# Which engine sums the last low column, casts the values and takes the stabilisers' low part in an fp32 attention

## What is computed

```
scores = jnp.einsum('bhqd,bhkd->bhqk', q, k) * scale
attn = jax.nn.softmax(scores, axis=-1)
out = jnp.einsum('bhqk,bhkd->bhqd', attn, v)
out = out.transpose(0, 2, 1, 3).reshape(b, s, H * DH)
out = out @ w_out.T + residual
```

## Time and profile before

| | |
|---|---|
| median of three runs | 4191.82 us |
| the profiled execution | 4191.36 us |
| its span, first to last instruction | 4189.6 us |
| TensorE matmul | 3758.9 us, 90% |
| VectorE | 3392.4 us, 81% |
| GpSimd | 3042.9 us, 73% |
| ScalarE | 2623.1 us, 63% |

### The profile page before, as it was taken

One profiled execution on the slowest core, in us unless ns is written; L12 is line 12 of the kernel. 1 busy time (PEld: TensorE's weight loads), 2 busy tenths in 40 slices (PEclk: granted clock), 3 DMA queues, 4 the chain that ended last, 5 costly groups with the idle time before them and its releaser, 6 DMA issues. The chain is left out here.

```text
span 4189.6 us, 55316 instructions
## 1 busy us (share of the span) xinstructions
PE 3758.9 (90%) x17018; PEld 2903.6 (69%) x17018; DVE 3392.4 (81%) x4389; ACT 2623.1 (63%) x3395; POOL 3042.9 (73%) x2832
## 2 busy tenths in 40 slices
PE   7949977869999999999999999999999999979563
PEld 4635545548888888888888888888888888857321
DVE  6845548869999999999999999999999999946511
ACT  6723333337777777777777777777777777733221
POOL 2456765758888888888888888888888888820155
PEclk9969998979999999999999999999999999989676
DMA  7123437852224332242322423224232242046295
GB/s 271 47 65 60 67 78 244 274 160 63 61 58 89 65 65 60 57 92 62 66 59 59 93 60 67 60 57 91 62 66 59 63 88 61 20 160 221 73 248 111
DMA packets 332634, 396.27 MB, mean 95 GB/s; under 512 B 142541, under 2 KB 251922, under 8 KB 319284
## 3 DMA queue, kind: packets, MB, share of 16 engines
q1 hardware_dynamic: 307702, 362.22, 33.9%
q0 software_dynamic: 24640, 30.52, 4.2%
HBM read 232.47 MB, written 117.79 MB: 84 GB/s over the span
## 5 line engine op out<-in xcount | busy, mean ns | idle before, releaser
L1815 ACT ACTIVATE at_ph<-at_ps_s 128x1024 fp32r<-128x1024 f32 x1024 | 1052.7, 1028 | 637.0 <-PE at_ps_s L1864 621.3
L1724 DVE TENSOR_REDUCE at_mx<-at_ps_u 128x2 f32<-128x1024 f32 x1016 | 1239.8, 1220 | 157.5 <-PE at_ps_u L1847 122.1
L1744 DVE TENSOR_TENSOR at_pl<-at_ps_s,at_ph 128x1024 fp32r<-128x1024 f32 x1024 | 1245.8, 1217 | 18.5 <-ACT at_ps_s L1818 17.4
L1818 ACT ACTIVATE at_ps_s<-at_ps_s 128x1024 f32<-128x1024 f32 x1024 | 1032.2, 1008 | 32.6
L1653 POOL TENSOR_TENSOR at_part<-at_ph,at_vl 128x512 f32<-128x512 f32 x768 | 799.0, 1040 | 114.2 <-ACT at_ph L1815 90.2
L1661 POOL TENSOR_TENSOR at_acc<-at_acc,at_part 128x512 f32<-128x512 f32 x640 | 833.5, 1302 | 50.1
L1879 PE MATMUL at_ps_v<-at_ph,at_va 128*128 128x512 f32 x2048 | 812.2, 397 | 1.1 <-DVE at_pl L1744 1.1
L1880 PE MATMUL at_ps_v<-at_pl,at_va 128*128 128x512 f32 x2048 | 812.9, 397 | 0.0
L1882 PE MATMUL at_ps_v<-at_ph,at_vx 128*128 128x512 f32 x1152 | 456.2, 396 | 0.0
L1880 PEld LDWEIGHTS at_ps_v<-at_pl,at_va 128*128 128x128 f32 x2048 | 387.4, 189 | 90.4
L1863 PE MATMUL at_ps_s<-q,k 128*128 128x512 f32 x1024 | 410.9, 401 | 21.6 <-DVE at_pl L1744 19.5
(11 more groups left out here) (285 smaller groups left out, 5446.3 us busy)
## 6 DMA issues: line engine op xcount, KB each, us to landing
wgu<-Wgu_in SPq DMA_DIRECT2D x64, 384.0 KB, 5.1
qT<-pj_rot SPq DMA_DIRECT2D x32, 512.0 KB, 5.2
vT<-pj_vo SPq DMA_DIRECT2D x16, 1024.0 KB, 5.7
kT<-pj_rot SPq DMA_DIRECT2D x32, 512.0 KB, 3.2
k<-kT SPq DMA_DIRECT2D x32, 512.0 KB, 11.6
q<-qT SPq DMA_DIRECT2D x32, 512.0 KB, 9.5
at_q<-at_low SPq DMA_DIRECT2D x128, 128.0 KB, 2.3
at_vf<-vT SPq DMA_DIRECT2D x32, 512.0 KB, 8.7
```

The lines of the kernel that those rows point to most:

```text
L1724: dve.tensor_reduce(mx[:, qb % 2, 2 * i:2 * i + 2], maxima_at(base, j)[:, 0:2], X, ALU.max).then_inc(s["u_max"], 1)
L1744: dve.tensor_tensor(pl[:, n % NP], ps_s[:, n % 2], ph[:, n % NP].bitcast(F32), ALU.subtract)\
L1815: act.activation(ph[:, n % NP], ps_s[:, n % 2], ACT.Exp, scale=DH ** -0.5)\
L1818: act.activation(ps_s[:, n % 2], ps_s[:, n % 2], ACT.Exp, scale=DH ** -0.5)\
```

## The change

There are four edits that belong together. (1) `SUMS` goes from 7 to 8: all even chunks are summed by GpSimd, slot 7 included, and `NX` from 9 to 8: TensorE has no second own product in slot 7. The `fold` of a block, the copy of its output and `whole` move back by one slot. (2) The casts to the high part of the values go from GpSimd to ScalarE, in slots 15, 17, 19 and 21. (3) The subtraction for `ml` goes from VectorE to GpSimd, into slot 2 of each block, behind a wait for VectorE's reductions. (4) The own products are prepared with one small copy instead of two.

```diff
-        SUMS = PER - 1
+        SUMS = PER
         NX = 2 * PER - SUMS
-        TAIL = 3
+        TAIL = 4
...
-                if c == KC - 2:
-                    return NX - 1
                 return c // 2 if c % 2 == 1 else None
...
-                def split_values(g, hh, half, i):
-                    if i == 0:
-                        pool.wait_ge(s[f"v{hh}"], half * 16 + 16)
-                        if g > 0:
-                            pool.wait_ge(s["pv_done"], g * SLOTS + (NP - SLOTS))
-                    at = slice(i * VQ, (i + 1) * VQ)
-                    pool.tensor_copy(va[:, hh, at, 0:DH], vf[:, hh, at]).then_inc(s["vh_ready"], 1)
...
-                    pool.tensor_copy(vx[:, hh, 0:NX - 1, 0:1], vl0[:, hh, 1::2].unsqueeze(2)).then_inc(s["vx_ready"], 1)
-                    pool.tensor_copy(vx[:, hh, NX - 1:, 0:1], vl0[:, hh, KC - 2:KC - 1].unsqueeze(2)).then_inc(s["vx_ready"], 1)
+                    pool.tensor_copy(vx[:, hh, :, 0:1], vl0[:, hh, 1::2].unsqueeze(2)).then_inc(s["vx_ready"], 1)
...
-                        if c < KC - 4:
+                        if c < KC - 2:
                             to = acc[:]
...
+                def low_stabilisers(block_):
+                    pool.wait_ge(s["mg_ready"], 2 * (block_ + 1))
+                    pool.tensor_tensor(ml[:, block_ % NQB], mg[:], mh[:, block_ % NQB].bitcast(F32), ALU.subtract)\
+                        .then_inc(s["nm_ready"], 1)
...
                         first_sums(g, hh, n)
-                        if n % PER == 5 and g * NQB + n // PER > 0:
+                        if n % PER == 2 and g * NQB + n // PER + 1 < HEADS * NQB:
+                            low_stabilisers(g * NQB + n // PER + 1)
+                        if n % PER == 6 and g * NQB + n // PER > 0:
                             whole((g * NQB + n // PER - 1) // NQB, (n // PER - 1) % NQB)
...
-                            if i % 2 == 0:
-                                split_values(nxt, 1 - hh, pr + hh, i // 2)
-                            else:
+                            if i % 2 == 1:
                                 low_values(nxt, 1 - hh, i // 2)
...
-                    dve.wait_ge(s["mg_ready"], 2 * (base * NQB + (qb + 1)))
-                    dve.tensor_tensor(ml[:, qb], mg[:], mh[:, qb].bitcast(F32), ALU.subtract).then_inc(s["nm_ready"], 1)
...
+                def split_values(g, hh, half, i):
+                    if i == 0:
+                        act.wait_ge(s[f"v{hh}"], half * 16 + 16)
+                        if g > 0:
+                            act.wait_ge(s["pv_done"], g * SLOTS + (NP - SLOTS))
+                    at = slice(i * VQ, (i + 1) * VQ)
+                    act.activation(va[:, hh, at, 0:DH], vf[:, hh, at], ACT.Copy).then_inc(s["vh_ready"], 1)
...
-                        if n % PER == 2 and n > PER:
+                        i = n % SLOTS - SLOTS // 2 + 1
+                        if 0 <= i < 2 * NQB and i % 2 == 0 and 2 * pr + n // SLOTS + 1 < HEADS:
+                            split_values(2 * pr + n // SLOTS + 1, 1 - n // SLOTS, pr + n // SLOTS, i // 2)
+                        if n % PER == 3 and n > PER:
                             output(pr * 2 + (n - PER) // SLOTS, (n - PER) % SLOTS // PER)
...
-                        if n % PER == 0 and g * NQB + n // PER > 0:
+                        if n % PER == 1 and g * NQB + n // PER > 0:
                             fold(g * NQB + n // PER - 1)
```

More of the change, by code:

```diff
@@ L1472, in sums_before @@
                 return n // PER * SUMS + sum(own_product(c) is None for c in range(2 * (n % PER)))
+            VQ = KC // NQB
             def loaded(eng, name, hh, half, each):
@@ L1597, in _ @@
                     link(pool.memset(k2[i][MROW:MROW + 2, :].bitcast(F32), -1.0))
-                VQ = KC // NQB
-                def split_values(g, hh, half, i):
-                    if i == 0:
-                        pool.wait_ge(s[f"v{hh}"], half * 16 + 16)
-                        if g > 0:
-                            pool.wait_ge(s["pv_done"], g * SLOTS + (NP - SLOTS))
-                    at = slice(i * VQ, (i + 1) * VQ)
-                    pool.tensor_copy(va[:, hh, at, 0:DH], vf[:, hh, at]).then_inc(s["vh_ready"], 1)
                 def low_values(g, hh, i):
@@ L1688, in head @@
                             own_products(nxt, 1 - hh)
+                low_stabilisers(0)
                 for i in range(NQB):
-                    split_values(0, 0, 0, i)
                     low_values(0, 0, i)
@@ L1819, in pair @@
                             .then_inc(s["pf_ready"], 1)
-                        if n % PER == 2 and n > PER:
+                        i = n % SLOTS - SLOTS // 2 + 1
+                        if 0 <= i < 2 * NQB and i % 2 == 0 and 2 * pr + n // SLOTS + 1 < HEADS:
+                            split_values(2 * pr + n // SLOTS + 1, 1 - n // SLOTS, pr + n // SLOTS, i // 2)
+                        if n % PER == 3 and n > PER:
                             output(pr * 2 + (n - PER) // SLOTS, (n - PER) % SLOTS // PER)
-                        elif n == 2 and pr > 0:
+                        elif n == 3 and pr > 0:
                             output(pr * 2 - 1, NQB - 1)
+                for i in range(NQB):
+                    split_values(0, 0, 0, i)
                 for pr in range(PAIRS):
@@ L1872, in values @@
                             pe.wait_ge(s["v_split"], g * NQB + NQB)
-                            pe.wait_ge(s["vx_ready"], 2 * (g + 1))
+                            pe.wait_ge(s["vx_ready"], g + 1)
                         if c2 == 0:
```

## The result

The changed kernel took 4465.94 us (4460.43 to 4475.94, 4 runs) beside 4191.28 us for the kernel before on the same chip: ratio 1.0656, 95% interval 1.0634 to 1.0678. The forecast was 4212 in a range from 4190 to 4252. The direction was right; the loss is 275 us where 21 were forecast.

The account below looks back on a forecast made before the run. TensorE bounds before, GpSimd after: about 6 us of first idle, 31 heads of 87.7 (2718.7) and a last of 80.5 sum to 2805.2, 21 us more than 2784.1; 4191.4 + 21 gives 4212 us, range 4190 to 4252.

Parts of the forecast that it names:

- GpSimd's sum of 87.7 us a head: GpSimd's work in an attention head after the change, if it never idles: 87.7 us, 0.7 more than today's head.
- The whole of attention: All 32 heads, first product to last addition: 2805.2 us after against 2784.1 before, 21 us more.
- The pair of product and addition: GpSimd's cost for one chunk in a block: forecast to stay at 2.56 us.
- its bounds: Stabilisers' low part on GpSimd: between 0 and 0.3 us beyond the gap each, 1.2 us a head at most.
- The casts on ScalarE: Four value casts a head, nearest row 382 ns: three hide in waits for TensorE, slot 19's can cost 0.2 to 0.4 us.
- TensorE's stalls fall from 2.9 us a head to about 1: TensorE in attention: stalls drop from 2.9 to about 1 us a head once VectorE's 0.16 to 1.1 us interruptions go.
- rival 1: Attention gets faster: GpSimd keeps up, TensorE stays the bound at 84.2 us a head, 4101 us in all; chance 6%.
- Why GpSimd won't idle: Attention, steady state: GpSimd falls about 7 us behind, ScalarE waits; late stabiliser rows hold TensorE 1 to 3 us in block 1.
- up to 3 us later: DMA queue: stabiliser rows leave up to 3 us later relative to ScalarE, just when TensorE wants them in slot 14.
- the forecast's 84.2 us: TensorE's head after the change: 83.2 us of matmuls and about 1 us of stalls.
- Rival 3: Waits add up instead of hiding, GpSimd idles in each head: 89.7 us a head, 83 more, 4275 us; chance 8%.
- The rules cited: VectorE with two SBUF inputs and GpSimd reading SBUF exclude each other; another rule keeps elementwise work off GpSimd, about twice as slow.

Follow-up runs that it names:

- e1: The changed kernel with the first stabiliser rows issued ahead of the q and k loads: 4223.68 us, 1.0058 of the kernel before.
- g10: The changed kernel with the store of block 2's output moved behind the operand loads, rows still behind the loads: 4223.18 us, 1.0054 of the kernel before.
- g5: The kernel before with only the value casts moved to ScalarE: 4182.08 us, 0.9981 of the kernel before.
- h1: The kernel before with the value casts on ScalarE and the first stabiliser rows ahead of the loads: 4182.82 us, 0.999 of the kernel before.
- h2: The kernel before with the stabilisers' low part on GpSimd and the first rows ahead of the loads: 4133.76 us, 0.9879 of the kernel before.
- e2: The changed kernel with the stabilisers' low part back on VectorE: 4353.22 us, 1.0368 of the kernel before.
- e3: The changed kernel with seven sums a block instead of eight: 4303.94 us, 1.0244 of the kernel before.

## Why the prediction was wrong

**What held.** GpSimd's sum of 87.7 us a head: 87.8 in the mean of e1 and of g10. The whole of attention in e1, from the first product (922.26) to the end of the last addition (3731.46), is 2809.2 us where 2805.2 were forecast. The pair of product and addition is still 2.56. The low part on GpSimd took 0.2 us, within its bounds, and a pair with it takes no longer than one without (1.43 us from addition to product, 2024.60 to 2026.03, after):

```profile
L1654 POOL TENSOR_TENSOR at_ml<-at_mg,at_mh x100: 191/200/212, 1008.3 to 3396.2; 128x4 fp32r<-128x4 f32 x100
...
DMA to landing us min/median/max: 1.9/2.0/11.1
```

The casts on ScalarE took 0.41 each (nearest row 0.38), and g5 and h1 show that with seven sums they cost nothing. VectorE's interruption of TensorE was real: h2 gains 52.7 us, 1.7 a head over 31 heads. The forecast had TensorE's stalls fall from 2.9 us a head to about 1. Over ten heads from 1000 us, counting the double gaps, where a record is missing, as two matmuls, the matmuls of both kernels start 0.234 us apart, and the longer gaps add up to 2.8 us a head before and 1.1 in h2. So rival 1's mechanism was right and its condition failed: it decides when GpSimd keeps up, and with eight sums GpSimd does not.

**The step that failed** is "Why GpSimd won't idle", where it came to the stabiliser rows. It looked at when they leave the queue ("up to 3 us later"), placed the trouble in slot 14, priced it at 1 to 3 us and let GpSimd's lag cover that. Measured, TensorE stalls 7.2 us a head at the start of block 1's scores, and GpSimd idles 8.7. In fact they left only 1.3 us later, and what counted was what stood ahead of them. The queue's list was read for its order, `ml`, low parts and outputs one behind the other, but not for this pair: the wait for the output sum, which the change itself makes late, and behind it 3.5 MB that start when that wait ends. The numbers were in the trace of before: the rows landed at 2059.38 + 3.3 = 2062.7, +18.3 us after the head's first exponential. TensorE asks for them at about +20 (after: 2080.90 - 6.66 = 2074.24, +19.8). Slack 1.5 us, and the forecast itself had GpSimd fall 7 us behind.

One rule fits a head of each of four kernels. The rows land 20.2 to 20.9 us after the first of the 3.5 MB is issued; TensorE wants them at +19.8 to +20.3. (Over the 78 long stalls of after, e2 and e3 between 1000 and 3400 us, TensorE goes on 20.4 to 22.0 us after that issue.)

| | first load, from the head's first exponential | rows land | TensorE's stall |
|---|---|---|---|
| before | -2.6 | +18.3 | none |
| e3 | +2.7 | +23.5 | 3.62 |
| e2 | +5.3 | +25.9 | 5.69 |
| after | +6.0 | +26.3 | 6.66 |

Nor did GpSimd's lag cover the stall, as that step said it would. When the scores stop for 6.7 us, the exponentials, the cuts and the maxima stop as well; GpSimd eats up its lag and then waits for the output's low half, the cut and the maxima (2.58, 2.23 and 3.04 in the head shown). In blocks 1 and 2 it is the slower one again and falls behind anew: ScalarE and the folds wait for its additions. A lag of 7 us carries nothing from one part of the head to the other, so the two bounds nearly add up where the forecast took the larger. As an estimate: TensorE alone, with the forecast's 84.2 us, the stall of 7.2 and the 2.2 of the clock (below), would take 93.6; the full sum, with GpSimd's 87.8, is 97.2; the mean head took 96.3. That reading rests on the order of the waits; e1 and g10 show only that all of it goes with the stall. Rival 3, at 8%, was this mechanism in general ("the late rows or the wait for the maxima let TensorE fall back so far that GpSimd idles in each head after all"). It was priced from the 2.0 us of an existing wait, when the price was on view in the queue: 8.7 us a head, not 2.0.

The clock adds to the stall. Behind it the matmuls start 0.43 us apart (2081.47, 2081.89) instead of 0.23 until about 2085, at the lower of the two levels: the granted clock from 2080.90 to 2085.10 is 0.51. Over the 25 heads this lasts 3.5 to 6.5 us and costs TensorE 1.4 to 3.0, 2.2 in the mean. The stretch has 0.95 of the full clock, e1 0.99. The forecast had no term for it.

**The rules cited.** With the Trainium skill, SBUF — State Buffer, "Who interferes with whom", the trace of before agrees. The subtraction on VectorE that took 1.06 us, from 1970.61 to 1971.67, lies in an addition on GpSimd and ends with it; the next, of 0.16 us, falls between two instructions there (GpSimd's timeline, then VectorE's):

```profile
1970.36 1.29 POOL L1661 TENSOR_TENSOR at_acc<-at_acc,at_part 128x512 f32<-128x512 f32 x1
...
1991.94 1.28 POOL L1661 TENSOR_TENSOR at_acc<-at_acc,at_part 128x512 f32<-128x512 f32 x1
1993.37 1.04 POOL L1653 TENSOR_TENSOR at_part<-at_ph,at_vl 128x512 f32<-128x512 f32 x1
...
1993.21 0.16 DVE L1737 TENSOR_TENSOR at_ml<-at_mg,at_mh 128x4 fp32r<-128x4 f32 x1
```

Of 28 between 1700 and 2300 us, the 14 that start 0.2 to 0.3 us into an addition take 1.05 to 1.12 us, and the 7 behind one take 0.16. In h2 all 113 on GpSimd take 196 to 204 ns. On the other side, the rule by which all of this would have been seen is in DMA: Bandwidth & Descriptors, "Queues, rings and completion order": each DMA engine takes descriptors in the order of its ring. The trace agrees: a 2 KB transfer took 10.0 us behind the 3.5 MB, of which the first was issued 10.2 us before it, and 2.0 in the median.

**What stays open.** What the 1.1 us of gaps a head that TensorE still has in h2 wait for. And why the loads are less late in e2 than in the changed kernel, and its stall varies from 2.6 to 6.4 us between heads: the low part on VectorE changes GpSimd's lag, but how wasn't tried by itself. Nor does a run separate what the lower clock costs in the changed kernel from what the stall does.

## What to carry to other kernels

In a queue that runs in order, a small transfer's latency is that of the bytes ahead of it: for each late wait in the queue, ask what large transfers it releases and which small ones stand behind them, and compute their slack from first issue to first use. An engine that falls behind by a harmless few microseconds moves all that waits for it, so price the lag at every place that waits for the engine, not only at the next one. Issue small transfers with a deadline ahead of bulk ones without; here that costs nothing when it isn't needed (0.9998) and only with it did the one part of the change that helps, the low part's move, show its 1.2%.

## What the runs showed of the hardware

- The 2 KB rows: 2.0 us from issue to landing in the median, 10.0 when 3.5 MB had been issued ahead of them in the 10.2 us before. The 3.5 MB kept the 16 DMA engines nearly full for about 18 us.
- One subtraction of 128 x 4 per block, on VectorE 161 to 1116 ns, holds TensorE up: four of them a head, at 0.5 us in the median, cost 1.7 us a head (h2 against before). On GpSimd the same subtraction takes 0.20 us. In the head of e1 shown it took 0.38 (2009.63 to 2010.01), beside a cut on VectorE from 2008.77 to 2009.96.
- After a stall of 6.7 us the matmuls started 0.43 instead of 0.23 us apart for the next 4 us, and the lower level followed each of the 25 long stalls of the changed kernel. In e3, with stalls of 2.8 to 4.3 us, the clock stayed at the full level after 13 of 27.
